# State products with queries in quadrants' blocks and states read in place, in a four-layer recurrent and attention model in fp32

## The chip, the cores and the metric

One core of one Trainium2 chip. The time is device time in microseconds of one launch. Engines in the profile: PE is TensorE, PEld its weight loads, DVE VectorE, ACT ScalarE, POOL GpSimd, SP the queue that issues most transfers.

## The reference

Three layers of a recurrent mixer on x (4 batches, 512 tokens, 512 channels), then one attention layer. Cut to what the change touches, one layer is:

```python
w = exp(-exp(time_decay + tanh(xw @ td_w1) @ td_w2)).reshape(b, l, h, 16)   # h = 32 heads
r, k, v = (xr @ Wr.T), (xk @ Wk.T), (xv @ Wv.T)                             # each (b, l, h, 16)
def step(s, rkvw):                        # s: (b, h, 16, 16)
    a = k_t[..., :, None] * v_t[..., None, :]
    out = einsum('bhi,bhij->bhj', r_t, u * a + s)
    s = a + w_t[..., :, None] * s
    return (s, out)
og = out.reshape(b, l, h, 16)             # normalised over the 16 of a head
og = ((og - mean) / sqrt(var + 1e-5)).reshape(b, l, e) * gn_w + gn_b
x1 = x + og * g @ Wo.T                    # g = silu(xg @ Wg.T)
```

A feed-forward with a token shift follows, then the next layer.

## The kernel before

A unit is one batch's 256 tokens in one layer: 3 layers x 4 batches x 2 halves = 24 units. Activations lie with channels on partitions, four tiles of 128 channels (k = 0 to 3) by 256 tokens; all is fp32, for which one matmul of the program is two records in the trace. The 256 tokens are cut into 32 chunks of 8. Inside a chunk the outputs are made in three levels of products ("leaf", levels 1, 2 and 4); the states between chunks come from updates (k by v per chunk), a scan over the 32 chunks on VectorE, and state products (query by state at the chunk's start) that are added to the own outputs.

The engines' programs are written out by hand. One step s of the main loop interleaves four units: n = s+1 (mixtures, LoRA, projections w, v, k, r, g), b = s (leaf, updates, scan, state products, group norm), c = s-1 (output product, second norm) and e = s-2 (feed-forward). PSUM banks go round in rings of named tiles: a_ring (three banks) for the unit n, b_ring (two) and o_ring (one) for b, c_ring (two) for c and e. A tile can be opened only when the tile three (or two, or one) places before it has been evicted. The tile w2r1 of the second pair of query and gate LoRA products comes three places behind v1.

Of unit b, before:

- `updates` (L783) makes U tiles of 32x32 products. ScalarE's `update` (L1211) evicts each of the eight into `s_in`, with a stride of four elements. `scan` (L1654) runs twice, over two channel tiles each (pair 0 and 1).
- `states_turned` (L1228) copies the states of one channel tile on ScalarE, chunk-major. `blocks` (L1671) multiplies them on VectorE by a block mask, so that each chunk has a 128x128 matrix with 16x16 blocks: two calls per channel tile, eight per unit, each 2048 elements a partition.
- `spread_queries` (L1184) writes the queries so that each of four token phases c has its own 256 columns with zeros between.
- `own_outputs` (L793) turns the own outputs to tokens on partitions, by four transposes on TensorE, into O0 or O1; `outputs` (L807) adds the state products there: 16 matmuls a call, eight calls a unit, 32 stationary and 128 moved columns.
- `group_mean`, `group_variance`, `group_scale` normalise O0 and O1 (512 elements each) into `oc`; `normed_back` (L818) turns them back on TensorE, `group_affine` (L1245) evicts with gn_w and gn_b, `gated` (L1699) multiplies by the gate.

VectorE's `mixed(n, "g")` (L1559), on which TensorE's gate projection waits, stands behind `group_mean(b, 0)`. ScalarE evicts the gate tiles g0 and g1 only when `gated(b, 1)` has read the old gate.

The value tiles `v_m` are laid out by four SP transfers for each pair (L493), behind the last update of the pair before.

Of the kernel before, what the change touches and what calls it, by code (L numbers as in the profile page):

```python
# [9 lines left out]
ALU = mybir.AluOpType  # L10
# [26 lines left out]
HALF = NC // 2  # L37
# [55 lines left out]
def other_tiles():  # L93
# [6 lines left out]
    for n in range(HEADS + LAG + 1):  # L100
        tiles += [(n // HPT - 1, "out", "dve")] if n % HPT == HPT - 1 and n >= HPT else []
        tiles += [(n - LAG, "t", "dve")] if 0 <= n - LAG < HEADS else []
        for b, name in beside(n):
# [11 lines left out]
           ("U03", "act"), ("U10", "act"), ("U11", "act"), ("U12", "act"), ("U13", "act"), ("N0", "act"), ("N1", "act")]  # L115
# [10 lines left out]
STATE_ACT = ["d0", "s0", "rz", "carry0", "t0", "t1", "d1", "s1", "carry1", "t2", "sq0", "t3", "std0", "sq1", "std1"]  # L126
STATE_DVE = ["scan0", "b00", "b01", "b10", "b11", "scan1", "sum0", "mean0", "b20", "b21", "var0", "b30", "b31", "sum1", "mean1", "rc0",
             "norm0", "var1", "rc1", "norm1", "og0", "og1"]
# [4 lines left out]
OUT_PE = ["b00", "b01", "b10", "b20", "b21", "b30"]  # L133

CONSTS = 11


def laid_out():

    at, n = {}, 0  # L140
    for name, size in [("blk", P), ("pick4", P), ("pars", LAYERS * PARS), ("s_first", KT * B * 32), ("s_now", KT * B * 32),
# [4 lines left out]
                       ("v_m", 2048), ("rz", 2 * 2048), ("d_in", PAIR), ("s_in", PAIR), ("s_turned", 2 * NC * 32), ("s_bd", 2 * HALF * P), ("oc1", 512)] + [  # L146
# [103 lines left out]
def build(nc, a):  # L250
    ctx = ExitStack()
    with ctx:
# [12 lines left out]
        eps = sb("eps", [P, 1])  # L265

# [55 lines left out]
        rz_flat = part_of("rz")  # L322
        rz = part_of("rz", "p (k c t) -> p k c t", k=KT, c=4)
        d_in = part_of("d_in", "p (k j c) -> p k j c", k=2, c=ROW)
        s_in = part_of("s_in", "p (k j c) -> p k j c", k=2, c=ROW)
        d_flat, s_flat = part_of("d_in"), part_of("s_in")
        s_turned = part_of("s_turned", "p (k c j) -> p k c j", k=2, c=NC)
        s_bd = part_of("s_bd", "p (a c e) -> p a c e", a=2, c=HALF)
# [22 lines left out]
        vm_loaded = sem("vm_loaded")  # L351
        a_ring = Ring(psum, (0, 1, 2), sem("a_ring_full"), {"act": sem("a_ring_act"), "dve": sem("a_ring_dve")}, by_unit(A_TILES))
# [12 lines left out]
        out_pe = Steps(sem("out_pe"), OUT_PE)  # L365
# [88 lines left out]
        def _(sp):  # L454
# [101 lines left out]
            for s in range(ITS + 2):  # L556
# [5 lines left out]
                if b < ITS:  # L562
                    load_vm(b, 1)
                if b == ITS:
# [36 lines left out]
        def _(pe):  # L601
# [186 lines left out]
            def own_outputs(it, pair):  # L788
                t = opened(o_ring, it, f"O{pair}").rearrange("p (k s c) -> p k s c", k=2, s=2)
                pe.wait_ge(leaf.sem, leaf.at(it, "o4d"))  # L790
                for i in range(2):
# [1237 lines left out]
```

## Time and profile before

| what | value |
|---|---|
| median of 3 runs | 3352.14 us (3348.86 to 3354.04) |
| span of the profiled execution | 3351.1 us |
| TensorE busy | 3201.9 us (96%) |
| VectorE busy | 2629.2 us (78%) |
| ScalarE busy | 1888.0 us (56%) |
| mean granted TensorE clock | 0.985 |

The profiled execution's own time is its span and about 1 us around it. The recurrent layers take up to about 2400 us, the attention the rest. In the layers the pattern repeats with each unit. Shares of busy time are shares of records' spans; TensorE's bars run into the next ones, so what a group of matmuls takes is read from the start of one group to the start of the next.

### The profile page before, as it was taken

What the parts mean: (1) busy time and instruction counts of PE and PEld (TensorE: products, weight loads), DVE (VectorE), ACT (ScalarE), POOL (GpSimd) and SP (SyncE); (2) the same over time, 40 slices, a digit from 0 to 9 for tenths busy, and PEclk for the clock granted to TensorE, in tenths of its full rate; (3) what the DMA queues carried; (4) which work ended last, traced back from release to release, by engine and by line L of the source; (5) the groups of instructions that cost most, each with busy time, mean ns of one, the idle gap of its engine ahead of it and who ended that gap; (6) DMA issues with size and microseconds to landing.
All of it is one profiled execution on the core that took longest, in us unless ns stands there. A gap on an engine that the chain in (4) does not pass through costs nothing.

```text
span 3351.1 us, 77435 instructions
## 1 busy us (share of the span) xinstructions
PE 3201.9 (96%) x33068; PEld 2386.8 (71%) x33068; DVE 2629.2 (78%) x3722; ACT 1888.0 (56%) x3119; POOL 226.1 (7%) x457
## 2 busy tenths in 40 slices
PE   6889999999999999999999999998999999998998
PEld 4667777777777777777777777776666666665666
DVE  3788888889888888888888898987457567566566
ACT  3556555556555555555655555555346656556555
POOL 0000000000000000000000000000101010010110
PEclk8889999999999999999999999999999999999999
DMA  3123332333333323333332233324324234133221
GB/s 126 58 77 106 120 111 90 117 133 114 114 105 118 111 90 119 117 121 110 114 114 102 98 121 123 105 105 159 107 57 116 51 76 112 31 89 103 63 69 48
DMA packets 91924, 336.82 MB, mean 101 GB/s; under 512 B 16704, under 2 KB 37824, under 8 KB 65600
## 3 DMA queue, kind: packets, MB, share of 16 engines
q0 software_dynamic: 39936, 234.91, 21.7%
q1 hardware_dynamic: 51216, 93.68, 8.8%
q8 instruction: 265, 4.34, 0.5%
q10 hardware_dynamic: 432, 3.28, 0.2%
q14 instruction: 75, 0.61, 0.1%
HBM read 252.11 MB, written 16.78 MB: 80 GB/s over the span
## 4 chain that ended last, share of the span: by engine, by line
PE 73%; DVE 22%; ACT 2%; issue 2%; DMA 1%; SPq 0%; DVEq 0%; ACTq 0%
PE psum L733 31%; PE psum L742 6%; DVE rw L1671 6%; PE psum L918 5%; PE psum L936 4%; DVE rw L1654 3%; PE psum L888 3%; PE psum L878 3%; PE psum L783 3%; PE psum L908 2%; DVE rw L1553 2%; DVE psum L1761 2%; PE psum L893 2%; DVE rw L1559 2%; PE psum L807 2%
## 5 line engine op out<-in xcount | busy, mean ns | idle before, releaser
L733 PE MATMUL psum<-rw 128*128 128x256 f32 x6144 | 1410.9, 385 | 11.5 <-DVE rw L1559 6.3
L733 PEld LDWEIGHTS psum<-rw 128*128 128x128 f32 x6144 | 1149.4, 191 | 215.0 <-issue 42.8
L1671 DVE TENSOR_TENSOR rw<-rw 128x2048 f32<-128x2048 f32 x192 | 433.0, 2287 | 34.3 <-PE psum L807 30.0
L1761 DVE CUSTOM_DVE_ANT_0 psum<-psum,mem 128x1024 f32<-128x1024 f32 x256 | 313.5, 1225 | 76.1 <-PE psum L908 75.8
L1309 ACT ACTIVATE rest<-psum,mem 128x1024 f32<-128x1024 f32 x256 | 284.9, 1113 | 90.8 <-DVE mem L1761 89.0
L918 PE MATMUL psum<-ident,rest 128*128 128x128 f32 x2048 | 270.5, 275 | 2.7 <-DVE mem L1720 1.6
L1211 ACT ACTIVATE rw<-psum 128x512 f32<-128x512 f32 x192 | 199.2, 1149 | 129.1 <-PE psum L783 129.1
L918 PEld LDWEIGHTS psum<-ident,rest 128*128 128x128 f32 x2048 | 235.2, 141 | 42.3 <-issue 14.7
L1553 DVE SCALAR_TENSOR_TENSOR rw<-psum,rw 128x256 f32<-128x256 f32 x480 | 196.2, 476 | 83.4 <-PE psum L699 43.5
L1948 POOL DMA_DIRECT2D rw<-big_dram x192 | 101.3, 529 | 2303.1 <-PE psum L733 2269.2
L742 PE MATMUL psum<-rw 128*128 128x512 f32 x432 | 221.5, 632 | 12.7 <-ACT rw L1173 7.9
L1302 ACT ACTIVATE mem<-psum 128x512 f32<-128x512 f32 x256 | 151.8, 594 | 141.9 <-PE psum L918 141.9
L908 PE MATMUL psum<-side 128*128 128x512 f32 x512 | 211.5, 494 | 12.8 <-ACT rest L1309 10.5
L1654 DVE TENSOR_TENSOR_SCAN rw<-rw 128x2112 f32<-128x2112 f32 x48 | 218.4, 4550 | 5.8 <-ACT rw L1211 5.8
L1104 ACT ACTIVATE rw<-rw 128x256 f32<-128x256 f32 x192 | 99.7, 590 | 216.5 <-DVE rw L1503 213.1
L1766 DVE COPY mem<-psum 128x512 f32<-128x512 f32 x256 | 175.8, 687 | 37.7 <-PE psum L918 37.7
L807 PE MATMUL psum<-rw 128*32 128x128 f32 x6144 | 196.3, 277 | 4.0 <-DVE rw L1671 4.0
L1228 ACT ACTIVATE rw<-rw 128x1024 f32<-128x1024 f32 x96 | 190.3, 2035 | 0.0
L807 PEld LDWEIGHTS psum<-rw 128*32 128x32 f32 x6144 | 162.7, 111 | 37.4 <-issue 26.9
L1641 DVE TENSOR_TENSOR rw<-psum,rw 128x512 f32<-128x512 f32 x168 | 113.6, 688 | 91.4 <-PE psum L742 89.0
L1963 POOL DMA_DIRECT2D side<-mem x256 | 123.3, 490 | 737.7 <-DVE mem L1737 622.5
L742 PEld LDWEIGHTS psum<-rw 128*128 128x128 f32 x432 | 74.3, 194 | 107.6 <-issue 82.2
(159 smaller groups left out, 4423.2 us busy)
## 6 DMA issues: line engine op xcount, KB each, us to landing
rw<-big_dram POOLq DMA_DIRECT2D x192, 1024.0 KB, 5.2
side<-mem POOLq DMA_DIRECT2D x256, 128.0 KB, 4.3
rw<-xs_dram SPq DMA_DIRECT2D x32, 512.0 KB, 3.5
side<-mem SPq DMA_DIRECT2D x256, 64.0 KB, 2.1
rw<-rw SPq DMA_DIRECT2D x192, 64.0 KB, 1.9
xs_dram<-rw SPq DMA_DIRECT2D x24, 512.0 KB, 5.3
rw<-x_dram SPq DMA_DIRECT2D x16, 512.0 KB, 3.7
mem<-xs_dram SPq DMA_DIRECT2D x16, 512.0 KB, 4.6
```

The costliest lines, as they stand in the source:

```text
L733: last = mm(t[:, o * TC:(o + 1) * TC], big[:, k, P * m:P * m + P], src[:, k, 0:TC], start=k == 0, stop=k == KT - 1, skip_group_check=True)
L742: b_ring.fill(mm(t, blk, src, start=True, stop=True), it, name)
L807: last = mm(t[32 * q:32 * q + 32, o, s, :], rz[:, k, c, 32 * m:32 * m + 32], s_bd[:, half, NM * i + m, :], start=False, stop=c == 3, skip_ ...
L908: last = mm(t[:, sh, :], q_side[group % 2][:, h, P * q:P * q + P].bitcast(F32R), k_side[group % 2][:, h, sh * 512:sh * 512 + 512].bitcast( ...
L918: last = nc.tensor.transpose(tokens(t, o), tokens(probs[:, n % HPT, :], first + o), ident[:])
L1211: b_ring.empty(f(to, t, ACT.Copy), it, f"U{pair}{q}")
L1228: state_act.inc(f(to, s_in[:, k % 2, :, 0:NC], ACT.Copy), it, f"t{k}")
L1309: s_ring.empty(f(probs[:, n % HPT, :].rearrange("p (a s) -> p a s", a=2), s_ring.bank(n, "s"), ACT.Exp, scale=-1.0, bias=mx[:, n % 8:n % 8 ...
L1553: last = stt(to[:, m, :], t[:, o * TC:(o + 1) * TC], par(layer, MAAS, KT * FAN[s] + m), sxa[:, m, :], ALU.add, ALU.mult)
L1654: state_dve.inc(nc.vector.tensor_tensor_scan(s_flat, d_flat, s_flat, 0.0, ALU.mult, ALU.add), it, f"scan{pair}")
L1671: state_dve.inc(tt(s_bd[:, half, :, :].rearrange("p c (h j) -> p c h j", h=4), own, place, ALU.mult), it, f"b{k}{half}")
L1761: maxima.inc(nc.vector.tensor_tensor_reduce(t, t, mbias.rearrange("p (a s) -> p a s", a=2), 1.0, 3.4e38, ALU.add, ALU.min, accum_out=mx[:, ...
```

## The change

The state products now have the queries as stationary and the scanned states as moved operand, read where the scan left them. A quadrant is 32 partitions, two heads.

1. `spread_queries` writes quadrant q's queries into the q-th of four blocks (`rz` by channel tile, token block, quadrant, token); the other quadrants' blocks are zero. Four writes of 1024 elements, each on 32 partitions.
2. `update` evicts each U tile in two parts, one for each head parity of the moved columns, each with a scale per partition, `own2`, that is one where the partition's head has that parity and else zero. There is one `s_in` for each pair. The initial states on the host have the same zeros.
3. `states_turned` and `blocks` are gone. `outputs` is called twice a unit, for half of the tokens each: 64 matmuls with 128 rows, 32 stationary columns (every fourth of a block of 128) and 32 moved columns (every 33rd element of `s_in`), each a sum of its own. The first waits for both scans. The outputs now stand by (channel tile, quadrant, chunk token) on partitions.
4. Own outputs come by 16 SP transfers of 32 partitions x 256 elements (`load_own`) into `ob`, and VectorE turns them in 32x32 blocks (`own_turned`, eight calls of 128 elements). `group_mean` first adds them to the state products.
5. After the norm, VectorE turns back (one call of 512 for each half); `group_affine` reads that in eight parts. Both TensorE turns (`own_outputs`, `normed_back`) are gone. Wg, Wo, gn_w and gn_b are permuted on the host.

```diff
+            def load_own(it):
+                sp.wait_ge(leaf.sem, leaf.at(it, "o4d"))
+                if it:
+                    sp.wait_ge(state_dve.sem, state_dve.at(it - 1, "own1"))
+                for k in range(KT):
+                    for q in range(4):
+                        sp.dma_start(ob[32 * k:32 * k + 32, q, :], o_leaf[32 * q:32 * q + 32, k, :]).then_inc(ob_loaded, 16)
...
                     load_vm(b, 1)
+                    load_own(b)
...
+            def outputs(it, half):
+                if half == 0:
                     pe.wait_ge(state_act.sem, state_act.at(it, "rz"))
+                    pe.wait_ge(state_dve.sem, state_dve.at(it, "scan1"))
+                t = opened(o_ring, it, f"O{half}")
+                queries = part_of("rz", "p (k m x) -> p k m x", k=KT, m=NM)
+                for m in range(4):
+                    for c in range(4):
+                        place = c * NM + 4 * half + m
+                        for k in range(KT):
+                            last = mm(t[32 * k:32 * k + 32, 32 * (4 * m + c):32 * (4 * m + c) + 32], queries[:, k, 4 * half + m, c:c + 125:4], s_in[k // 2][:, k % 2, :, place],
+                                      start=True, stop=True, skip_group_check=True)
+                o_ring.fill(last, it, f"O{half}")
...
+                for q in range(4):
+                    rows = slice(32 * q, 32 * q + 32)
+                    last = f(rz[rows, :, :, q, :], hm["r"][rows, :, :].rearrange("p k (m x) -> p k m x", m=NM), ACT.Copy)
...
             def update(it, pair, q):
-                b_ring.empty(f(to, t, ACT.Copy), it, f"U{pair}{q}")
+                for h in range(2):
+                    last = f(to[:, h], t[:, h], ACT.Identity, scale=own2[:, h:h + 1])
+                b_ring.empty(last, it, f"U{pair}{q}")
...
+            def own_turned(it, half):
                 if half == 0:
+                    dve.wait_ge(ob_loaded, 16 * 16 * (it + 1))
+                t = ob[:, :, HALF_TOKENS * half:HALF_TOKENS * half + HALF_TOKENS].rearrange("p q (m l c) -> p m c q l", m=4, c=4)
+                to = own_t[half].rearrange("p (m c q l) -> p m c q l", m=4, c=4, q=4)
+                for m in range(4):
+                    last = nc.vector.transpose(to[:, m], t[:, m])
+                state_dve.inc(last, it, f"own{half}")
+            def group_mean(it, half):
+                t = filled(o_ring, it, f"O{half}")
+                dve.wait_ge(state_dve.sem, state_dve.at(it, f"own{half}"))
+                o_ring.empty(tt(oc[half], t, own_t[half], ALU.add), it, f"O{half}")
...
+                state_dve.inc(nc.vector.transpose(own_t[pair], oc[pair]), it, f"back{pair}")
```

TensorE's queue between the first update of pair 1 and the second value tile, before. L618 and L641 belong to the norm of unit c, L733 is a projection, L712 and L722 are the two decay products:

```order
L783 MATMUL psum<-rw 32x4x32 x32
L618 MATMUL psum<-rw,ones 32x256 x4
L733 MATMUL psum<-rw 128x256 x8
L712 MATMUL psum<-rw 64x128 x8
L807 MATMUL psum<-rw 32x128 x16
L722 MATMUL psum<-rw 128x128 x8
L641 MATMUL psum<-rw 128x256
L807 MATMUL psum<-rw 32x128 x16
```

The same place now (line numbers have moved: L792 updates, L627 and L650 the norm, L742 projection, L721 and L731 the decay products):

```order
L792 MATMUL psum<-rw 32x4x32 x32
L627 MATMUL psum<-rw,ones 32x256 x4
L742 MATMUL psum<-rw 128x256 x8
L721 MATMUL psum<-rw 64x128 x8
L731 MATMUL psum<-rw 128x128 x8
L650 MATMUL psum<-rw 128x256
```

Both single state products have left; the decay products stand next to each other.

TensorE's queue at the end of a step, from the variance sums of unit c (L624), before. L793 and L818 are transposes, L807 state products, the rest projections and L630 the spread of the deviation:

```order
L624 MATMUL psum<-rw,ones 32x64 x16
L733 MATMUL psum<-rw 128x256 x24
L793 MATMUL psum<-ident,rw 128x128 x4
L807 MATMUL psum<-rw 32x128 x32
L630 MATMUL psum<-rw,pick 32x64 x16
L733 MATMUL psum<-rw 128x256 x8
L807 MATMUL psum<-rw 32x128 x32
L733 MATMUL psum<-rw 128x256 x8
L818 MATMUL psum<-ident,rw 128x128 x4
```

The same place now, L808 being the new state products:

```order
L633 MATMUL psum<-rw,ones 32x64 x16
L742 MATMUL psum<-rw 128x256 x24
L808 MATMUL psum<-rw 32x32 x64
L639 MATMUL psum<-rw,pick 32x64 x16
L742 MATMUL psum<-rw 128x256 x8
L808 MATMUL psum<-rw 32x32 x64
L742 MATMUL psum<-rw 128x256 x32
```

All state products of a unit stand in two groups of 64 now, behind key and first query tile and behind the second query tile. Just ahead of L624 in both kernels stand the two pairs of query and gate LoRA products (L698, L699; now L707, L708); the 32 state products between the pairs are gone.

VectorE's queue between the value mixture and the key mixture (L1559), before:

```order
L1559 TENSOR_TENSOR rw<-rw 128x1024
L1713 TENSOR_TENSOR rw<-rw,psum 128x512
L1715 TENSOR_TENSOR rw<-rw 128x512
L1713 TENSOR_TENSOR rw<-rw,psum 128x512
L1715 TENSOR_TENSOR rw<-rw 128x512
L1671 TENSOR_TENSOR rw<-rw 128x2048 x4
L1559 TENSOR_TENSOR rw<-rw 128x1024
```

And now (L1520 the mixtures, L1670 and L1672 the last sums of unit e, L1624 the turns of own outputs):

```order
L1520 TENSOR_TENSOR rw<-rw 128x1024
L1670 TENSOR_TENSOR rw<-rw,psum 128x512
L1672 TENSOR_TENSOR rw<-rw 128x512
L1670 TENSOR_TENSOR rw<-rw,psum 128x512
L1672 TENSOR_TENSOR rw<-rw 128x512
L1624 STREAM_TRANSPOSE rw<-rw 128x128 x8
L1520 TENSOR_TENSOR rw<-rw 128x1024
```

Eight short turns stand where four long block products stood; the four others stood between the group means and the second norm of unit c.

## Rows read from the trace of the kernel before

**Rows 1.** Stretches: length, busy PE, PEld, DVE, ACT, POOL, clock, DMA share, GB/s.
```profile
1110.50:1206.60 96.10, 95.63 (x1058) 74.37 (x1059) 85.29 (x112) 55.71 (x90) 4.21 (x8) 1.00 0.32 112
...
2263.00:2376.80 113.80, 93.37 (x913) 67.71 (x906) 87.05 (x104) 56.49 (x83) 2.63 (x5) 0.88 0.35 126
```

**Rows 2.** Chain that ended last, pieces in order of time: start, us, what.
```profile
1114.23 0.44 PE psum L818 x4
...
1167.20 0.44 PE psum L793 x4
...
1173.97 1.01 PE psum L807 x32
...
1176.70 1.01 PE psum L807 x32
...
1192.85 0.60 DVE rw L1675
...
1203.90 1.13 DVE rw L1503
```

**Rows 3.** Timeline of TensorE in that step: start, us, line, shapes [idle before].
```profile
1145.23 1.96 PE L742 MATMUL psum<-rw 128*128 128x512 f32 x4 [0.34 <-ACT rw L1173]
...
1183.44 1.95 PE L807 MATMUL psum<-rw 128*32 128x128 f32 x64
...
1186.38 0.65 PE L624 MATMUL psum<-rw,ones 128*32 128x64 f32 x32
1186.97 10.85 PE L733 MATMUL psum<-rw 128*128 128x256 f32 x48
1197.66 0.60 PE L793 MATMUL psum<-ident,rw 128*128 128x128 f32 x4
...
1199.96 0.63 PE L630 MATMUL psum<-rw,pick 128*32 128x64 f32 x32
1200.52 3.72 PE L733 MATMUL psum<-rw 128*128 128x256 f32 x16
1204.17 1.95 PE L807 MATMUL psum<-rw 128*32 128x128 f32 x64
1206.22 1.56 PE L733 MATMUL psum<-rw 128*128 128x256 f32 x6
```

**Rows 4.** TensorE's groups by line and shape: busy us, mean ns of one.
```profile
L807 PE MATMUL psum<-rw 128*32 128x128 f32 x6144 | 196.3, 277 | 4.0 <-DVE rw L1671 4.0
...
L783 PE MATMUL psum<-rw 32*32 32x128 f32 x6144 | 112.6, 275 | 10.4 <-DMA rw<-rw 8.5 <-DVE rw L1641 1.5 <-issue 0.5
...
L624 PE MATMUL psum<-rw,ones 128*32 128x64 f32 x1536 | 33.1, 229 | 13.9 <-ACT rw L1098 13.9
```

**Rows 5.** Timeline of VectorE in that step.
```profile
1170.02 4.49 DVE L1671 TENSOR_TENSOR rw<-rw 128x2048 f32<-128x2048 f32 x2
...
1183.64 1.66 DVE L1553 SCALAR_TENSOR_TENSOR rw<-psum,rw 128x256 f32<-128x256 f32 x4 [1.30 <-PE psum L699]
```

**Rows 6.** ScalarE's groups: 1024 elements with a stride (L1228) and dense.
```profile
L1228 ACT ACTIVATE rw<-rw 128x1024 f32<-128x1024 f32 x96 | 190.3, 2035 | 0.0
...
L1201 ACT ACTIVATE rw<-rw 128x1024 f32<-128x1024 f32 x96 | 96.3, 1052 | 2.2
```

**Rows 7.** Timeline of ScalarE, last two updates and eviction of v1.
```profile
1182.48 2.08 ACT L1211 ACTIVATE rw<-psum 128x512 f32<-128x512 f32 x2 [2.95 <-PE psum L783]
1184.33 0.66 ACT L1169 ACTIVATE rw<-psum 128x512 f32<-128x512 f32 x1
```

**Rows 8.** SP's timeline, and the landing times of L493's transfers.
```profile
1159.43 2.54 SPq L493 DMA_DIRECT2D rw<-rw  x4
...
DMA to landing us min/median/max: 1.9/1.9/8.3
```

**Rows 9.** VectorE's block products: in the last step, and in all.
```profile
2322.54 9.09 DVE L1671 TENSOR_TENSOR rw<-rw 128x2048 f32<-128x2048 f32 x4
...
L1671 DVE TENSOR_TENSOR rw<-rw 128x2048 f32<-128x2048 f32 x192 | 433.0, 2287 | 34.3 <-PE psum L807 30.0 <-ACT rw L1228 2.6 <-ACT rw L1236 1.1
```

More of the change, by code:

```diff
@@ L786, in updates @@
                     b_ring.fill(last[i], it, f"U{pair}{q}")
[L788 to L791, printed above, removed]
-                    for s in range(2):
-                        mm(t[:, i, s, :], tokens(o_leaf[:, 2 * pair + i, :], s), ident[:], start=i == 0 and s == 0, stop=False, is_transpose=True, skip_group_check=True)
@@ L795, in outputs @@
-            def outputs(it, k, half):
-                pair, o = k // 2, k % 2
-                if k == 0 and half == 0:
-                    pe.wait_ge(state_act.sem, state_act.at(it, "rz"))
-                t = o_ring.bank(it, f"O{pair}").rearrange("p (k s c) -> p k s c", k=2, s=2)
-                pe.wait_ge(state_dve.sem, state_dve.at(it, f"b{k}{half}"))
-                for i in range(2):
-                    c = 2 * half + i
-                    for s in range(2):
-                        for q in range(4):
-                            m = 4 * s + q
-                            last = mm(t[32 * q:32 * q + 32, o, s, :], rz[:, k, c, 32 * m:32 * m + 32], s_bd[:, half, NM * i + m, :], start=False, stop=c == 3, skip_group_check=True)
-                if o == 1 and half == 1:
-                    o_ring.fill(last, it, f"O{pair}")
-                else:
-                    out_pe.inc(last, it, f"b{k}{half}")
@@ L1051, in _ @@
                 if has_b:
-                    outputs(b, 3, 0)
-                    outputs(b, 3, 1)
+                    outputs(b, 1)
                 if s == ITS - 1:
@@ L1236, in group_deviation, with group_affine @@
                 state_act.inc(f(gstd[pair], gstd[pair], ACT.Sqrt, scale=1.0 / S, bias=eps[:]), it, f"std{pair}")
-            def group_affine(it, pair):
+            def group_affine(it, half):
                 layer = layer_of(it)
-                t = filled(b_ring, it, f"N{pair}")
-                if pair == 0 and it:
+                act.wait_ge(state_dve.sem, state_dve.at(it, f"back{half}"))
+                if half == 0 and it:
                     act.wait_ge(c_ring.full, c_ring.full_at(it - 1, "wo1"))
-                for o in range(2):
-                    k = 2 * pair + o
-                    last = f(ogc[:, k, :], t[:, o * TC:(o + 1) * TC], ACT.Identity, scale=par(layer, GNW, k), bias=par(layer, GNB, k))
-                b_ring.empty(last, it, f"N{pair}")
+                t = own_t[half].rearrange("p (m c q l) -> p q m l c", m=4, c=4, q=4)
+                to = ogc.rearrange("p q (h m l c) -> p q h m l c", h=2, m=4, c=4)
+                for q in range(4):
+                    last = f(to[:, q, half], t[:, q], ACT.Identity, scale=par(layer, GNW, q), bias=par(layer, GNB, q))
+                state_act.inc(last, it, f"aff{half}")
             def feed(it, s, n):
@@ L1653, in scan @@
                 dve.wait_ge(state_act.sem, state_act.at(it, f"s{pair}"))
[L1654 to L1656 removed]
+                state_dve.inc(nc.vector.tensor_tensor_scan(s_flat[pair], d_flat, s_flat[pair], 0.0, ALU.mult, ALU.add), it, f"scan{pair}")
+            def own_turned(it, half):
                 if half == 0:
[L1659 to L1671 removed]
```

158 lines of the change are left out of this document (50 added, 108 removed).

## Prediction

> **What bounds the kernel now.** Read the stretches first [rows 1]. In the layers the work repeats every 96.1 us, one step per unit, and in the step shown TensorE is busy for 95.63 of 96.10 us at a granted clock of 1.00 (the 2.4 GHz level). VectorE is busy for 85.29, ScalarE for 55.71. So time is won in a step only where TensorE's queue gets shorter and nothing else becomes late in the same place. The last such step has no projections of a next unit beside it: there TensorE does 93.37 of 113.80 us and VectorE sets the pace. Then read the chain [rows 2]: between about 1183 and 1206 us it runs on VectorE, through the block products of L1671, although TensorE is full there too. The two are level at the end of a step. Last, TensorE's timeline [rows 3] shows what stands between the projections, and that is what the change takes away. Its bars overhang the next start by up to 0.3 us, so I subtract starts, or use the chain's pieces.
>
> **What leaves TensorE before the pair of query and gate LoRA products.** The turns of normed outputs (L818) cost two times 0.44, the first turn of own outputs (L793) 0.44, and the two single state products 1.01 each [rows 2]: 3.34 us. Against it: the second decay product (L722) needs the tanh of the first. State products lay between them; now they meet. The same pattern, an eviction by ScalarE between two groups with nothing between, cost 0.34 us (the row at 1145.23 in [rows 3]). Net 3.0 us.
>
> **What leaves in the rest of the step.** Call t the moment when the first query and gate products are full, 1183.6 us (VectorE starts on them at 1183.64 [rows 5]). Before, 1.95 us of state products run there, until the second pair of these products starts (the row at 1183.44 in [rows 3]). They filled a wait. The second pair needs the third bank of the ring, which holds value tile v1, and ScalarE evicts v1 only after two update evictions, at 1184.33, 0.55 us long: free at t+1.3 [rows 7]. The change also splits each update eviction in two, with a scale per partition. Two evictions took 1.85 us (start to start) [rows 7]; I give the split 2.4 (between no more, and twice as much). Then v1 is free at t+1.85, and the second pair starts 1.9 us after t: of the 1.95 us removed nothing is left. Adding 1.0 for the pair (from 1185.39 to 1186.38) and 0.6 for L624, keys and first queries start at t+3.5 (before: 1186.97, t+3.4) and, after 10.7 us [rows 3], end at t+14.2 (before t+14.1). A second tie holds the same place: the second key tile needs the bank of the first tile of that second pair, which VectorE empties only behind its second scan, at about t+7; so an earlier start of the pair would not help either.
>
> From t+14.2, X is the time of one half of the new state products, 64 matmuls, 128 records. First half until T0 = t+14.2+X. Then L630 and queries, 0.57+3.65 [rows 3], and the second half, X. The gate's projection may start at t+18.4+2X. Before it started at 1206.22, t+22.6. On VectorE the mean of the first half now waits for T0, the product of the gate's mixture stands behind it, and TensorE waits for that: five 512-element operations at 0.6 (one of them ScalarE's square), 0.2 for the scale, two 1024-element ones at 1.13 [rows 2], and 0.3 for hand-overs: T0+5.8. With 4.2+X on TensorE's side VectorE is later only for X under 1.6.
>
> **X.** No row shows 32 moved columns. The nearest [rows 4]: L807 with 128 columns and 32 output partitions, 196.3 us for 6144 records, 32.0 ns; L624 the same with 64 columns, 33.1 us for 1536, 21.5 ns over the run and 18 where it isn't held up (0.59 us for 32 records, 1186.38 to 1186.97 [rows 3]). The slope gives 11 to 12 ns for 32. But both operands are now strided: a query column every 4th element, a state every 33rd. On ScalarE 1024 elements with such a stride cost 2035 ns against 1052 dense [rows 6], so 32 strided columns may cost like 64. I take 18 ns, X = 2.3. Ends: 11.4 (X = 1.5) and 24.8 (X = 3.2, both operands slow and in part one after the other).
> The Trainium skill speaks of strides too ("SBUF — State Buffer", on cachelines: each access to a new 16-byte line pays). It also names a floor of about 25 ns from one matmul to the next ("TensorE: Matmul & The Clock Gate", Part 1); a matmul here is two records, so that rule permits 12.5 ns a record and X = 1.6, and L783's 112.6 us for 6144 records, 18.3 ns [rows 4], doesn't break it.
>
> **The sum.** A steady step saves 3.0 + 22.6 - 18.4 - 2X = 7.2 - 2X: 2.6 us at X = 2.3, 0.8 at X = 3.2; at X = 1.5 VectorE's side gives 3.0 + 22.6 - 21.5 = 4.1. 23 steps: 60, 18 and 94 us. The last step: VectorE drops eight block products, a 24th of 433.0 us, 18.0 [rows 9], of which the first four end at 2331.6; it gains eight turns of 128 elements (0.3 each, from 1024 in 1.13 plus a start: 2.4), two adds and two turns of 512 (2.4), and waits for the second scan's state products and ScalarE's square (4). About 9 us. Together 69 us. The profiled span is 3351.1, the median of the runs 3352.14, so 1.0 lies around it: 3352.1 - 69 = 3283.
>
> **Costs put at nothing, and their cover.** (1) SP now issues 16 transfers of own outputs behind the four of the value tile. Four took 2.54 us from 1159.43 [rows 8], so the 16 end at 1172.1, and with 1.9 to landing [rows 8] they are in at 1174. VectorE arrives there at 1170.02 [rows 5] and waits 4 us; eight turns to 1176.4, then 2.3 us of other work (mixture, centring) that must be done before t, which is then about 1181: slack 2.3. Behind them on SP stand the store of x and the next load of x1, 2 us later, both wanted tens of us later. (2) The query spreading now makes ScalarE write 1024 elements on 32 partitions four times, 4.2 against 2.1 us; two state turnings of 1.95 go from the same place. (3) VectorE's tail after the second half grows by an add and two turns, and ScalarE's gate eviction and level 1 wait for it: p0 is ready some 13.3 us after the gate's projection starts, TensorE asks at 14.5.
>
> **Rivals.**
> *A. All of TensorE's saving arrives* (ScalarE's split costs nothing, the filled waits are covered by drift): 3.34 + 1.95 + 4.35 - 2X = 5.0 at X = 2.3 (4.35 is 2.30 from 1197.66 to 1199.96 and 2.05 from 1204.17 to 1206.22 [rows 3]): 23 times, plus 9: 3228. Against it: v1's release has a row.
> *B. Strided operands keep the old pace or worse.* At r ns a record the step saves 7.2 - 0.256 r; with the last step's 9 us the sum is zero at r = 30. At 35 ns a step loses 1.8, the kernel 31 us: 3383, slower than before. For it: ScalarE's factor of two, if both operands are read one behind the other. Against it: a weight load of 32 columns is hidden at 18 ns in L624.
> *C. Own outputs land late.* The same kind of transfer has landed in 1.9 us at the median and 8.3 at most [rows 8]; each us beyond a slack of 2.3 delays t. If 16 issues cost 0.9 us each, or the landing drags to 6 us, a step loses 1.7 to 2 more: 3325. It decides from a landing at 1176.5.
> *D. It moves but doesn't pay*: the head and tail waits (tanh, v1, the mean before the gate's mixture) are each 0.5 to 1 us longer than costed: saving near 0.3 a step, 3337 to 3352.
>
> **Chances.** Forecast (3250 to 3322) 0.58; A 0.10; B 0.10, of it 0.05 slower, 0.03 same; C 0.12, of it 0.03 slower, 0.02 same; D 0.10, of it 0.03 slower, 0.04 same. The range from 3235 to 3345 leaves out most of A and the slow ends. A measurement tells this kernel from no change by about 0.2%, 7 us: faster 0.80, same 0.09, slower 0.11.
>
> **What would show it.** TensorE idle for 1.5 to 2 us before the second query and gate pair, released by ScalarE's v1 eviction, and 0.3 to 0.4 before L722's group: the first two steps. Records of the new state products 18 ns apart (11 and 25 the ends, 30 rival B). VectorE idle some 6 us before the first half's mean, and no more L1671. VectorE waiting about 4 us on a transfer ahead of its eight turns (over 6: rival C). A period of 93.5 us instead of 96.1, the last step 9 us shorter. I am wrong if the period is under 91.5 or over 95.5.

## The result and the profile after

The changed kernel takes 3420.8 us at the median (3415.9 to 3428.0, 4 runs) against 3350.8 (3348.9 to 3354.0, 4 runs) for the kernel before, run beside it: a ratio of 1.0209, 95% interval 1.0194 to 1.0225. It is 2.1% slower. I had forecast 3283, 69 us faster than 3352; it is 69 us slower. The profiled execution has a span of 3414.1 us against 3351.1.

Where the 63 us of span lie is read from VectorE's scans, which mark each step. From the second scan of the second step to that of the 23rd there are 21 steady steps: 227.24 to 2242.40 us before, 229.28 to 2311.61 after, that is 95.96 us a step before and 99.16 after. So the steady steps cost 67 us, and the ends give 4 back. One step of the kernel before, as a stretch (columns as in [rows 1]):

```profile
1089.50:1185.21 95.71, 95.25 (x1064) 74.01 (x1056) 84.90 (x112) 55.31 (x89) 4.21 (x8) 1.00 0.32 112
```

And three of the changed kernel:

```profile
526.03:622.61 96.58, 90.56 (x1042) 69.79 (x1043) 72.31 (x117) 52.60 (x97) 4.22 (x8) 1.00 0.34 117
1217.30:1318.76 101.46, 95.25 (x1042) 73.22 (x1042) 72.32 (x117) 52.60 (x97) 4.21 (x8) 0.95 0.32 110
1714.02:1813.79 99.77, 93.68 (x1042) 72.15 (x1043) 72.32 (x117) 52.65 (x97) 4.21 (x8) 0.97 0.32 112
```

At a granted clock of 1.00 TensorE's work did shrink, from 95.25 to 90.56 us a step, and VectorE's from 84.90 to 72.31. But TensorE is now idle for 6.0 us of the step instead of 0.5, and the step of 96.58 us is 0.6 us over the mean of before. And most steps are not at 1.00: with the same count of matmuls the step at 0.95 has TensorE busy for 95.25 us. Two things went wrong, then: waits that eat the whole saving and 0.6 us more, and a lower clock (the other 2.6 us of the 3.2). The split is rough: one other step, from 1119.7 us, is at 1.00 too and lasts 97.59 us; the run fill_fit below gives 2.3 us for the clock.

The waits of TensorE over the whole execution (who waited, for whom, us in total, times, longest):

```profile
PE psum L742 <- DVE rw L1469: 63.4, 22, 2.9
PE psum L707 <- ACT rw L1143: 36.8, 23, 1.6
```

The second row is the wait for the eviction of v1 that the prediction expected. The first row was not expected, and has no counterpart in the kernel before. TensorE has finished the gate's projection and comes to the next step's first work, the receptance product of the feed-forward, whose input is the mixture that VectorE writes in L1469. The chain of waits in a step at clock 1.00 shows how that mixture comes to be late (start, us, what):

```profile
1138.67 2.34 PE psum L808 x108
...
1141.03 0.70 DVE rw L1630
...
1142.69 0.69 DVE rw L1637
...
1143.68 0.70 DVE rw L1648
...
1144.41 0.72 DVE rw L1650
...
1145.16 2.12 ACT rw L1210 x4
1147.27 0.22 ACT rw L1200
...
1147.90 0.70 DVE rw L1648
...
1149.26 1.64 DVE rw L1469 x4
...
1150.95 7.17 PE psum L742 x32
```

From the second half's first add (L1630, 1141.03) to the end of the mixture 9.9 us pass. TensorE has 7.2 us of gate projection to cover that (1140.89 to 1148.06) and then stands still for 2.9. In the chain are the two pieces that the change added, the turn of the first half back (L1650) and ScalarE's affine of it (L1210, 2.12 us), and the second half's square root (L1200) is queued behind that affine. The mixture itself needs neither: it only stands behind the second half's group scale in VectorE's order.

The granted clock in pieces of 0.5 us, around two gaps of TensorE, the one just ahead of the step from 1714.02 and the one inside it (same columns; the clock is the third last):

```profile
1711.50:1712.00 0.50, 0.50 (x8) 0.38 (x4) 0.00 (x0) 0.50 (x2) 0.00 (x0) 1.00 1.05 147
1713.00:1713.50 0.50, 0.00 (x0) 0.00 (x0) 0.50 (x2) 0.50 (x2) 0.00 (x0) 1.00 0.93 393
1715.50:1716.00 0.50, 0.50 (x14) 0.41 (x3) 0.50 (x1) 0.50 (x1) 0.00 (x0) 1.00 0.00 0
1716.50:1717.00 0.50, 0.50 (x2) 0.34 (x1) 0.50 (x1) 0.00 (x0) 0.00 (x0) 0.50 0.00 0
1718.50:1719.00 0.50, 0.50 (x2) 0.41 (x2) 0.50 (x3) 0.32 (x1) 0.00 (x0) 0.50 0.00 0
1719.50:1720.00 0.50, 0.50 (x4) 0.43 (x3) 0.50 (x2) 0.00 (x0) 0.00 (x0) 1.00 0.00 0
1746.00:1746.50 0.50, 0.03 (x1) 0.03 (x1) 0.50 (x3) 0.50 (x3) 0.00 (x0) 1.00 0.98 393
1748.00:1748.50 0.50, 0.50 (x2) 0.34 (x2) 0.50 (x2) 0.00 (x0) 0.00 (x0) 0.50 0.37 148
1751.00:1751.50 0.50, 0.50 (x4) 0.42 (x3) 0.50 (x2) 0.50 (x2) 0.00 (x0) 1.00 0.00 0
```

TensorE stands still at 1713 (the wait for v1), works again from 1713.9, and from 1716 runs at 0.50, the 1.2 GHz level, for 3.4 us; half a microsecond then holds two of its matmul records instead of four. The same behind the wait for the mixture, which ends at 1746.47. Such a fall stands behind the LoRA pairs in 18 of the 21 steady steps and behind the wait for the mixture in 12. The kernel before has none at either place. It has one in its 21 steps, near 1460 us, and so has every kernel below but all_own in the same step; the counts below leave it out. That one stands behind a wait too: the updates of L783 wait there for the transfers that lay out the value tile, as TensorE's timeline of the kernel before shows.

```profile
1457.15 1.17 PE L783 MATMUL psum<-rw 32*32 32x128 f32 x64 [2.04 <-DMA rw<-rw]
```

In that step this wait is 2.0 to 4.4 us long in all 14 kernels, and the clock falls from 0.6 us before its end to 2.2 us behind it in all but all_own. Why the transfers land late just there is open.

What came out as forecast: there is no L1671 any more, and L808's records, here in TensorE's groups of the changed kernel:

```profile
L808 PE MATMUL psum<-rw 128*32 128x32 f32 x6144 | 112.3, 248 | 2.6 <-issue 2.6
```

112.3 us for 6144 records is 18.3 ns (against 32.0 of L807 in [rows 4]).

### The profile page after: what moved, and what is told of

Read it like the earlier page. It is cut to its first block, busy times and chain, and to the rows that moved or that the text cites. A ratio compares the mean times of both kernels' runs of the same rounds, so it can differ in the third digit from the quotient of the medians.

```text
span 3414.1 us, 77104 instructions
## 1 busy us (share of the span) xinstructions
PE 3145.0 (92%) x32684; PEld 2330.3 (68%) x32684; DVE 2327.4 (68%) x3819; ACT 1822.0 (53%) x3311; POOL 226.0 (7%) x457
## 4 chain that ended last, share of the span: by engine, by line
PE 77%; DVE 12%; ACT 6%; DMA 2%; issue 2%; SPq 1%; DVEq 0%; ACTq 0%
PE psum L742 34%; PE psum L751 6%; PE psum L909 4%; PE psum L927 3%; PE psum L879 3%; PE psum L808 3%; PE psum L869 3%; PE psum L792 3%; PE psum L899 2%; DMA rw<-rw 2%; DVE psum L1718 2%; PE psum L884 2%; ACT rw L1210 2%; PE psum L695 2%; PE psum L675 1%
## 5 line engine op out<-in xcount | busy, mean ns | idle before, releaser
L742 PE MATMUL psum<-rw 128*128 128x256 f32 x6144 | 1461.0, 396 | 73.0 <-DVE rw L1469 63.4
L742 PEld LDWEIGHTS psum<-rw 128*128 128x128 f32 x6144 | 1196.1, 198 | 292.3 <-DVE rw L1469 72.8
L1143 ACT ACTIVATE rw<-psum 128x512 f32<-128x512 f32 x192 | 113.4, 603 | 272.0 <-PE psum L742 271.7
L1186 ACT ACTIVATE rw<-psum,own 128x256 f32<-128x256 f32 x384 | 208.4, 714 | 84.5 <-PE psum L792 84.5
L1630 DVE TENSOR_TENSOR rw<-psum,rw 128x512 f32<-128x512 f32 x48 | 33.2, 691 | 215.8 <-PE psum L808 215.8
L1602 DVE TENSOR_TENSOR rw<-psum,rw 128x512 f32<-128x512 f32 x168 | 113.6, 688 | 90.6 <-PE psum L751 88.2
L751 PEld LDWEIGHTS psum<-rw 128*128 128x128 f32 x432 | 74.4, 194 | 110.1 <-issue 82.9
L927 PE MATMUL psum<-mem 128*32 128x128 f32 x4096 | 129.3, 280 | 16.9 <-DVE mem L1723 15.5
L1624 DVE STREAM_TRANSPOSE rw<-rw 128x128 f32<-128x128 f32 x192 | 58.2, 374 | 126.3 <-DMA rw<-rw 126.3
```

Of the source, the lines that this page charges most:

```text
L742: last = mm(t[:, o * TC:(o + 1) * TC], big[:, k, P * m:P * m + P], src[:, k, 0:TC], start=k == 0, stop=k == KT - 1, skip_group_check=True)
L751: b_ring.fill(mm(t, blk, src, start=True, stop=True), it, name)
L927: last = mm(t[AD * h:AD * h + AD, 0:P], v, probs_t[:, st, h, :], start=st == 0, stop=st == ST - 1, skip_group_check=True)
L1186: last = f(to[:, h], t[:, h], ACT.Identity, scale=own2[:, h:h + 1])
```

## Experiments

The kernels below differ from the changed one by the edits shown. The theory was now: (1) the late mixture costs the step 2.5 to 2.9 us, (2) each gap of TensorE also brings its clock down for a while. Rivals: something else of VectorE's tail is as late as the mixture; the clock answers to the small matmuls of L808 and L792, not to the gaps; own outputs that land late hold up the step. "Steady step" below is the mean of the 21 steps, measured as above, and "falls" counts those of them with a clock fall at the first and at the second place (in no_gaps and all_own the first place is the wait right behind the LoRA pairs, ahead of L633). Not in the table are falls elsewhere: two in fill_both, one each in fill_fit and mix_own, three in closed_dense.

| kernel | median us | ratio to before (95%) | steady step | falls |
|---|---|---|---|---|
| before | 3350.8 | 1 | 95.96 | 0, 0 |
| changed | 3420.8 | 1.0209 (1.0194 to 1.0225) | 99.16 | 18, 12 |
| fill_v1 | 3418.9 | 1.0204 (1.0187 to 1.0221) | 99.24 | 0, 16 |
| fill_both | 3429.0 | 1.0234 (1.0218 to 1.0251) | 100.18 | 0, 0 |
| fill_fit | 3362.8 | 1.0033 (1.0021 to 1.0046) | 96.90 | 0, 0 |
| mix_early | 3341.2 | 0.9971 (0.9961 to 0.9981) | 95.86 | 19, 0 |
| v1_first | 3407.6 | 1.0166 (1.0149 to 1.0184) | 98.61 | 10, 13 |
| mix_own | 3341.5 | 0.9967 (0.9956 to 0.9978) | 96.06 | 17, 0 |
| mix_fill | 3309.6 | 0.9879 (0.9864 to 0.9894) | 94.37 | 0, 0 |
| no_gaps | 3348.4 | 0.9993 (0.9983 to 1.0003) | 96.23 | 21, 0 |
| all_own | 3321.4 | 0.9911 (0.9895 to 0.9926) | 95.81 | 21, 0 |
| closed | 3246.1 | 0.9692 (0.9675 to 0.9709) | 92.11 | 0, 0 |
| closed_out | 3229.2 | 0.9639 (0.9624 to 0.9653) | 91.32 | 0, 0 |
| closed_dense | 3222.2 | 0.9617 (0.9603 to 0.9632) | 90.98 | 0, 0 |

**Idle-time matmuls in the gaps.** They do nothing but keep TensorE busy while it would wait:

```diff
+            def filler(it, count):
+                if it >= 0:
+                    pe.wait_ge(*o_ring.empty_at(it, "O1"))
+                for _ in range(count):
+                    mm(psum[:, 5, 0:256], ident[:], pick[:, 0:2, :], start=True, stop=True, skip_group_check=True)
...
                     lora_two(n, 0)
+                    if has_b:
+                        filler(b - 1, 7)
                     lora_two(n, 1)
```

> The changed kernel with seven idle-time matmuls (128x256, their result is read by nobody) between the two pairs of query and gate LoRA products, where TensorE otherwise waits 1.60 us for ScalarE's eviction of value tile v1. Theory 1 (the gap itself is what the granted clock answers to): in the trace of the changed kernel the clock falls to the 1.2 GHz level within 3 us behind this wait in 19 of 21 steady steps, for 3.4 to 7 us, and a second time behind the wait for the feed-forward mixture in 12. With the gap filled the first falls go, about 1.8 us a step; the second stay: 3421 - 19 x 1.8 = 3387. Theory 2 (the small state products of L808 or L792 lower the clock, or it falls whatever stands there): no change, 3421 within 7 us. Theory 3 (the filler only costs): 3421 + 21 x 0.3 = 3427.

> As before, and twelve more such matmuls behind the gate's projection, where TensorE waits 2.9 us for VectorE's mixture (L1469). Both gaps are filled, nothing is removed from any queue and no wait is shortened. Theory 1 (gaps bring the clock down): every steady step runs at 1.00 and lasts what the one undisturbed step of the changed kernel lasts, 96.6 us, instead of 99.2 on average: 3421 - 21 x 2.6 = 3366. What is left over the 95.96 of the kernel before is then waits alone. Theory 2 (not the gaps): 3421.

Measured: 3418.9 and 3429.0. In fill_v1 no fall is left at the first place, and 16 at the second. In fill_both there is none at either. The clock did as (2) says; the times didn't (3387 and 3366 were expected), because the fillers were twice as long as meant. A record takes 0.225 us and a matmul is two records: 3.15 us of filler in a gap of 1.6 us made the queue 1.55 us longer, about what the clock gave back, and in fill_v1 four more steps fell at the second place. So once more at the right size, three and six matmuls:

> The fillers again at the right size: an idle-time matmul is two records of 0.225 us, which the two runs before counted as one, so they were twice as long as the gaps. Now three of them (1.35 us) in the gap of 1.60 us and six (2.70 us) in that of 2.9 us, for both gaps of the changed kernel. Theory 1 (a gap brings the clock down, nothing else): all steady steps at 1.00 and 96.6 to 97 us long instead of 99.2: 3421 - 21 x 2.4 = 3371. Theory 2 (the steps of the oversized filler were at 1.00 because TensorE had still more to do, not because the gaps were closed): falls remain in at least half of the steps, over 3395.

Measured: 3362.8, 58 us less than the changed kernel, with more work in TensorE's queue. A steady step of fill_fit:

```profile
611.61:707.80 96.19, 94.68 (x1060) 73.16 (x1060) 72.31 (x116) 52.63 (x97) 4.21 (x8) 1.00 0.33 116
```

94.68 us busy is the 90.6 of the changed kernel at full clock and 18 filler records. The second rival is out: the small matmuls are all there, and the clock holds in 19 of the 21 steps. Of the 3.2 us a step that the change loses, the clock is 2.3 by this run (99.16 - 96.90).

**The mixture earlier on VectorE.**

```diff
                 if has_c:
                     norm_c(c, "sx")
+                    norm_c(c, "mixr")
                 if has_b:
                     group_scale(b, 1)
...
-                    norm_c(c, "mix")
+                    norm_c(c, "mixk")
```

> The changed kernel with one move on VectorE: the receptance mixture of the feed-forward (mixr) stands ahead of the second half's group scale instead of behind it, with the key mixture still behind. Theory 1 (the wait of L742 for L1469 is the step that the prediction missed): the mixture ends 2.5 us earlier, TensorE's wait of 2.9 falls to 0.4 us, 21 x 2.5 = 52 us, and with it the second fall of the clock in a step (12 of 21 steps, 1.8 us each: 22): 3347. Rival (something else of VectorE's tail, the first product p0 or the gate's eviction, is as late): the wait moves to L751 and less than 15 us are won: over 3406.

Measured: 3341.2, 80 us less than the changed kernel and 10 less than the kernel before; so nothing else of VectorE's tail is as late (the first rival). TensorE's waits in mix_early now read:

```profile
PE psum L707 <- ACT rw L1143: 36.8, 23, 1.6
...
PE psum L742 <- DVE rw L1469: 11.1, 22, 0.5
```

The wait fell from 2.9 to 0.5 us, no other took its place, and the clock does not fall behind 0.5 us. One line of order decided whether this change is a gain or a loss. A step at full clock is 94.19 us here, the first of these two stretches of mix_early:

```profile
228.24:322.43 94.19, 90.61 (x1042) 69.82 (x1044) 72.41 (x117) 52.53 (x97) 4.22 (x8) 1.00 0.34 119
802.92:898.62 95.70, 91.96 (x1042) 71.08 (x1042) 72.42 (x116) 52.52 (x97) 4.21 (x8) 0.98 0.34 116
```

19 of the 21 are like the second row, with the fall behind the wait for v1.

**The price of that one fall.** The three fillers at the first place, on top of mix_early:

> mix_early with the three idle-time matmuls in the gap of 1.60 us between the LoRA pairs, nothing else. No wait is shortened: this prices the clock alone. In mix_early the clock fell in 19 of 21 steady steps, on average 95.6 us long against 94.2 undisturbed. Theory: 3341 - 19 x 1.4 = 3314, clock 1.00 in the steady steps. Rival (the gain of closed is all from queue order): 3341.

Measured: 3309.6, 32 us less than mix_early, for 19 falls: 1.7 us a fall. The steady step is 94.37 us.

**v1 evicted first.** On ScalarE `stream(n, "v", 1)` moves ahead of `update(b, 1, 2)` and `update(b, 1, 3)`, from the changed kernel:

> The changed kernel with one move on ScalarE: value tile v1 is evicted ahead of the last two update evictions instead of behind them. The LoRA pair's wait of 1.60 us goes. The second tie that the prediction named (the second key tile needs a bank that VectorE empties only behind its second scan) should hold: 1.8 us of wait appear between the two key tiles, and the queue is no shorter. If any gap of that size brings the clock down: 3421 within 7. If it is the gap among the light matmuls ahead (32-row LoRA products and 32x32 updates) that does: falls go in 19 steps, 3387. Rival (the second tie does not hold): 3421 - 21 x 1.6 - 34 = 3353.

Measured: 3407.6, between the times that were expected. The wait of 1.6 us for ScalarE is gone, but a wait of up to 1.2 us for VectorE is in its place, as TensorE's waits in v1_first show:

```profile
PE psum L707 <- DVE rw L1514: 27.6, 24, 1.2
...
PE psum L742 <- DVE rw L1514: 8.3, 12, 1.2
```

The second pair of LoRA products also needs the bank of the first pair's first product, and VectorE must have emptied that. This is a third tie at the same place, ahead of the one that the prediction named. The named one is the second row: in the 11 steps without a fall at the first place, the second key tile waits 0.65 us for VectorE. Behind the gap of 1.2 us the clock fell in 10 steps of 21, behind that of 1.6 in 17 to 19.

**Own outputs.** The eight turns move on VectorE to the place just ahead of the first half's mean, on top of mix_early:

> One move on top of mix_early: VectorE's eight turns of own outputs stand right ahead of the first half's mean instead of ahead of the key mixture, where VectorE waits 5 us for the sixteen transfers. This prices the transfers' landing. The prediction's first cost put at nothing: the wait is inside VectorE's slack (in the changed kernel it still waits 1.9 us for TensorE before the query and gate mixing), so 3341 within 5, and L1624 waits for no transfer any more. Rival (the landing at 5 to 6 us delays what VectorE does next and through it TensorE): 1 us a step less, 3320.

Measured: 3341.5 against 3341.2. In the changed kernel VectorE waits 126.3 us for these transfers, 5.5 us a step; in mix_own it waits for none of them, and nothing is gained. The wait costs nothing.

**Real work in the gap.** On top of mix_early, TensorE does the last updates between the two LoRA pairs, v1 is evicted first, and VectorE's second scan goes behind the mixing:

```diff
                 if has_n:
+                    lora_two(n, 0)
+                if has_b:
+                    updates(b, 1, 1)
+                if has_n:
-                    lora_two(n, 0)
                     lora_two(n, 1)
...
-                if has_b:
-                    scan(b, 1)
                 if has_n:
                     mixing(n, "rg", 1)
+                    mixed(n, "r")
+                if has_b:
+                    scan(b, 1)
```

> Real work in place of the gap instead of filler, on top of mix_early: TensorE does the last two updates of pair 1 between the two pairs of query and gate LoRA products instead of ahead of both; ScalarE evicts v1 ahead of them; VectorE does the second query and gate mixing and the query mixture ahead of its second scan. Nothing is added or left out. Theory: the LoRA pair's wait of 1.6 us goes (mix_early: 36.8 us in 23 waits) and no bank stands behind the scan any more; without gaps the clock stays at 1.00 (1.4 us a step in mix_early: 95.6 on average against 94.2 in its two undisturbed steps, 19 times: 27 us): 3341 - 37 - 27 = 3277, a period of 92.5 us. Rival 1 (the scan, now 3 us later, makes the first half of the state products or the feed-forward's norm late): a wait of 1 to 3 us ahead of L808 or L639, and a clock fall with it: 3310 to 3345. Rival 2 (clock falls don't go with the gap): 3304.

Measured: 3348.4, no gain and 71 us over what was expected. It went as rival 1 says, though for another reason than the later scan: the pair waits for next to nothing now (2.8 us in the whole execution), but the norm (L633) right behind it does, for a square that ScalarE does behind the updates (TensorE's waits in no_gaps):

```profile
PE psum L633 <- ACT rw L1073: 53.6, 26, 5.0
```

1.9 us a step, and the clock falls behind it in all 21 steps. Then with three further moves (the turns late, the first decay product ahead of the value tile, the second square root ahead of the affine):

> no_gaps with three more moves: the turns of own outputs late as in mix_own; the first decay product ahead of the value stream's first tile, so that its tanh lies beside that tile (0.38 us a step of wait in mix_early); the second half's square root ahead of the first half's affine on ScalarE (2.1 us earlier, so that VectorE's group scale of the second half waits no more). Expected from no_gaps: 21 x 0.38 = 8 for the decay wait, up to 0.4 x 21 = 8 for what the mixture is still late: 3277 - 8 - 8 = 3261. If TensorE's queue alone sets the pace (90.6 us busy at 1.00), the least that this order can give is 95.96 - 90.6 = 5.4 us a step against the kernel before: 3352 - 21 x 5.4 - 9 = 3230. Rival: something late takes the place of each: 3277 or more.

Measured: 3321.4, from no_gaps 27 less (19 between the two profiled executions, where the 21 steady steps give 9, the wait for the tanh having been 0.38 us a step, and what lies ahead of them 11). Expected were 3261. The 1.9 us ahead of L633 and the 21 falls are still there. The last move takes them away:

```diff
                 if has_n:
                     stream(n, "v", 1)
+                if has_c:
+                    norm_c(c, "sq")
                 if has_b:
                     update(b, 1, 2)
                     update(b, 1, 3)
...
-                if has_c:
-                    norm_c(c, "sq")
```

> all_own with one more move: ScalarE's square for the feed-forward's norm stands ahead of the last two update evictions instead of behind them. In no_gaps and all_own the gap of 1.6 us ahead of the second LoRA pair had only moved behind it: 1.9 us ahead of L633, which waits for that square, and the clock fell behind it in all 21 steady steps (period 95.5, TensorE busy 92). Theory (the clock follows the gap wherever it stands): without it the clock stays at 1.00, and both go: 1.9 + 1.5 us a step, 21 x 3.4 = 71, 3321 - 71 = 3250, a period of 92. Rival 1 (another gap over 1 us takes its place): 3285 or more. Rival 2 (the clock also falls where TensorE has no gap, from the light matmuls L707, L792, L633 in a row): 3321 - 21 x 1.9 = 3281, falls in most steps.

Measured: 3246.1, 75 us less than all_own. One ScalarE instruction of 1.06 us, 2.1 us earlier, gives 3.7 us a step: the wait of 1.9, and 1.8 that are put down to the clock. A steady step of closed:

```profile
490.27:582.29 92.02, 90.30 (x1042) 70.02 (x1041) 72.49 (x116) 52.36 (x96) 4.23 (x8) 1.00 0.35 121
```

**State products earlier.** On top of closed:

```diff
                     stream(n, "k", 1)
-                    stream(n, "r", 0)
                 if has_b:
                     outputs(b, 0)
+                if has_n:
+                    stream(n, "r", 0)
...
-                if has_n:
-                    stream(n, "r", 1)
                 if has_b:
                     outputs(b, 1)
+                if has_n:
+                    stream(n, "r", 1)
```

> closed, and on TensorE each half of the new state products one projection tile earlier (the first ahead of the first query tile, the second ahead of the second). VectorE then has the group norm's chain 3.6 us earlier; it waits 7 us for the first half now. The mixture (0.5 us late in mix_early and all_own) would be done before it is wanted: 21 x 0.5 = 10 us less than closed, 3240. Rival (the scan ends at most 1 us before the earlier place, or the second half waits for VectorE to empty its one bank): a new wait ahead of L808 of 1 us or more, no gain or a loss of 20.

Measured: 3229.2, 3.6% faster than the kernel before and the fastest one that computes the same outputs. The wait for the mixture is gone from the list of waits, and TensorE is idle for 0.9 us of a step of closed_out:

```profile
490.15:581.07 90.92, 89.98 (x1042) 70.02 (x1041) 72.56 (x117) 52.20 (x96) 4.22 (x8) 1.00 0.35 123
```

**What the strides cost.** From closed, each state product reads 32 neighbouring columns of either operand; the right states are left out of the output.

> closed with wrong operands in the state products: 32 query columns and 32 state columns next to each other instead of every 4th and every 33rd, the same count of matmuls and results. This leaves the right states out of the output and prices the strides alone. In the changed kernel a record of L808 took 18.3 ns, as the prediction took it, and a half 2.3 us. If the strides cost what the prediction feared from ScalarE's row (a factor of up to two): 12 ns a record and 1.5 us a half, 1.5 us a step, closed less 30. If a record of this shape has a floor of its own: closed within 7.

Measured: 3222.2, 24 us less than closed. The groups of L808, matmuls and weight loads, of closed:

```profile
L808 PE MATMUL psum<-rw 128*32 128x32 f32 x6144 | 112.0, 248 | 6.0 <-issue 5.6 <-DVE rw L1632 0.4
L808 PEld LDWEIGHTS psum<-rw 128*32 128x32 f32 x6144 | 104.7, 155 | 21.7 <-issue 21.0 <-DVE rw L1632 0.6
```

The same of closed_dense:

```profile
L808 PE MATMUL psum<-rw 128*32 128x32 f32 x6144 | 63.3, 198 | 6.8 <-issue 6.0 <-DVE rw L1632 0.6
L808 PEld LDWEIGHTS psum<-rw 128*32 128x32 f32 x6144 | 57.7, 110 | 22.6 <-issue 21.9 <-DVE rw L1632 0.8
```

A record takes 10.3 ns dense and 18.2 strided; a matmul and a weight load are each some 50 ns longer with strides. At 8 ns for each of 256 records the queue is 2.0 us a step shorter, of which 1.1 arrive (92.11 - 90.98): TensorE now waits up to 0.7 us for VectorE's gate mixture ahead of the gate's projection, the limit that the prediction gives for an X under 1.6, and three steps have a clock fall, each behind an idle stretch of 2.0 to 2.3 us inside L639's group.

## Why the prediction was wrong

**The part before t**: right. The wait for the tanh is 0.38 us in the changed kernel (0.34 taken).

**The tie at the LoRA pair**: right in size. Forecast idle for 1.5 to 2 us, released by ScalarE's eviction of v1; measured 1.60. The split updates of two tiles take 1.9 us from start to start (2.4 taken, 1.85 before), so the pair starts 1.5 us behind t instead of 1.9.

**X**: right. 18.3 ns a record (18 taken), halves of 2.26 and 2.34 us (2.3). It rested on ScalarE's factor of two for strides, and closed_dense bears such a factor out for TensorE (18.2 against 10.3 ns). Without strides X would be 1.3, just under its low end of 1.5. The Trainium skill, which the prediction weighed there, names lines of 16 bytes, each new one of which costs ("SBUF — State Buffer", on cachelines); the trace agrees that strided operands cost, 8 ns a record. Its floor of about 25 ns from one matmul to the next ("TensorE: Matmul & The Clock Gate", Part 1) is not seen here: the two records of one matmul take 20.6 ns dense, and the measurement decides.

**The sum of a step**: "7.2 - 2X: 2.6 us". With the mixture moved and the clock held (mix_fill) the steady step is 94.37 us against 95.96: 1.6 of the 2.6 are saved, and the rest of the wait for the mixture, 0.5 us, is half of what is missing. The undisturbed steps of mix_early are 94.2. What was computed on TensorE's queue arrived to within 1 us.

**The failed step is cost (3)**: "VectorE's tail after the second half grows by an add and two turns, and ScalarE's gate eviction and level 1 wait for it: p0 is ready some 13.3 us after the gate's projection starts, TensorE asks at 14.5". The sum for p0 was near the truth (in the step above it is ready after 14.4 us, 1155.26 - 1140.89), but p0 is not the first thing that TensorE asks of VectorE. Ahead of it in the queue stands the feed-forward's product, which asks for the mixture 7.2 us after the gate's projection starts, and the mixture is ready after 10.0. Before, the same operation was done in time. VectorE's timeline of the kernel before, the second mean and the mixture:

```profile
1206.19 0.69 DVE L1675 TENSOR_REDUCE rw<-psum 128x32 f32<-128x512 f32 x1
...
1211.44 3.25 DVE L1508 SCALAR_TENSOR_TENSOR rw<-rw 128x256 f32<-128x256 f32 x8
```

And the product of the feed-forward that wants it, in TensorE's timeline:

```profile
1214.11 7.07 PE L733 MATMUL psum<-rw 128*128 128x256 f32 x32
```

The mean began with the gate's projection (1206.22), and the mixture's four operations, half of the row of L1508, ended some 6.9 us later. The product came 7.9 us behind the start of the projection, because the two groups of turns (L818, 0.44 each) that the change removes stood in between. The change took 0.7 us of cover away and put 3 us into the chain. I checked one consumer of the tail instead of each in the order in which TensorE comes to them. mix_early shows that this alone, with the clock falls behind that wait, turns the result's sign: -80 us.

**The second failure is a term that was not there**: the clock. The prediction forecast an idle stretch of 1.5 to 2 us in each step and priced it at its own length. Behind it stands a clock fall worth 1.7 us (mix_fill), and the gap for the mixture brings a second one. In the changed kernel this is 2.3 us a step, some 48 of the 138 us between forecast and result. No rival held it. The rows read ahead of the prediction do hold the hint: in the last step, the one with waits, the clock is 0.88, in the full steps 1.00 [rows 1].

**The other two costs at nothing** held. The transfers of own outputs land after 3.2 us at the median, not 1.9, and VectorE waits 5.5 us instead of 4, but it is then early at the query and gate mixing anyway (1.9 us of waiting for TensorE there), and mix_own gains nothing. Rival C is out: its sign, a wait of over 6 us, was nearly met, but 1.9 us of the slack of 2.3 are left. Rival B is out (18.3 ns, it decides at 30), and so is A. Rival D had a late tail in mind, but at the gate's mixture, where TensorE waits for nothing (its projection starts at 1140.89, as the state products end), and it priced its waits at 0.5 to 1 us.

**The last step** and what stands behind it: the period is 1.4 us shorter, and from its end to the end of the span it takes 4.8 less: 6.2, forecast 9.

So: of the 138 us between 3283 and 3421, the mixture's wait and its falls explain 80 (mix_early), the falls at the first place 32 (mix_fill). Of the 27 us that are left between mix_fill and the forecast some 21 are 1 us a steady step (94.37 against 95.96 - 2.6), half of it the rest of the mixture's wait; the other half was not traced.

## What to carry to other kernels

When a queue gets shorter, list every later wait of that engine in the order of its queue, and give each its own slack: the first consumer that asks decides, not the last of the chain. An idle stretch on TensorE is not free at its own length: in these runs a wait of 1.6 us in each step cost 3.3, its own length and 1.7 us of clock, and harmless work put in its place won the 1.7 us back. If an edit removes small work that stood between two dependent groups, move other work into that place in the same edit; here nine moves of order (all those of closed_out) made a gain of 3.6% out of a loss of 2.1%. The same moves in the kernel before were not tried; TensorE is idle there for 0.5 us of a step at 1.00, so that they have little to win in its steady steps.

## What the runs showed of the chip

- Filling a gap with work that is thrown away can make a kernel faster: fill_fit does 4.05 us more on TensorE in each step and is 58 us faster.
- Behind waits of 0.2 to 0.5 us at these places the granted clock fell in no steady step, behind 1.2 us in 10 of 21, behind 1.6 in 17 to 19, behind 1.9 in all 21 (no_gaps, all_own). The fall began between 1.6 us before the gap's end and 2.1 us behind it, also in work that was dense again, and the clock stayed at the 1.2 GHz level for 3.4 or 6.8 us. The Trainium skill ("TensorE: Matmul & The Clock Gate", on oscillation in real kernels) tells of the same pattern, waits that return the clock to its low level again and again; its waits for transfers are 3 to 5 us long, and this trace shows the pattern with waits of 1.2 to 2.9.
- The length of the gap does not decide alone. Ahead of the updates (L792) the 14 kernels have 26 idle stretches of 1 to 2 us in other steady steps than the one near 1400, and only four have a fall behind them (two in fill_both, one in fill_fit, one in mix_own); of the 14 of 2.0 to 4.4 us in that one step 13 have. What differs between the places, and what activity the chip asks for, was not tried.
- A gap that is closed at one place reappears at the next tie, and the clock falls there as before (no_gaps: L633). It paid to close the last of them: 75 us (all_own to closed).
- 32 columns with a stride in both operands cost 18.2 ns a record against 10.3 dense.
- One step near 1400 us is 3 to 7 us longer in every kernel, before too. It holds the wait of 2.0 to 4.4 us for the value tile's transfers and, but in all_own, a clock fall behind it. What stays open is why these transfers land late there (up to 8.3 us in the kernel before, against 1.9 at the median).
